# Attention and experts of one layer on one core: the order of score pairs and side operations on TensorE, and the staging of the last expert rounds

## The reference, cut to what matters

```python
Q, K = _apply_rope(Q), _apply_rope(K)                      # 16 heads of 8
scores = einsum('bhqd,bhkd->bhqk', Q, K) / sqrt(8)
attn = softmax(where(causal, scores, -inf))
x = _layernorm(x + (attn @ V) @ o_proj_weight.T)
y = x + _msa(_layernorm(x, ln1_w, ln1_b), w_qkv, w_proj)   # full attention, 16 heads
h = _layernorm(y, ln2_w, ln2_b)
one_hot = one_hot(argmax(h @ gate_w + gate_b), 8)
y = y + sum over e of one_hot[:, e] * (gelu(h @ w1[e]) @ w2[e])   # 128 -> 512 -> 128
out = _layernorm(x + y)
```

## Time and profile before

| | us |
|---|---|
| median of the runs | 973.14 (972.72 to 976.86) |
| the profiled execution | 974.19 |
| its span, first to last instruction | 972.4 |
| first exp to last exp | 41.9 to 873.6 |
| behind the last exp | 98.8 |
| ACT busy | 779.5, of it exps 741.6 |
| ACT idle in front of exps | 87.3 |
| PE busy | 847.0 |

### The profile page before, as it was taken

The page is one execution under the profiler, slowest core; times in us unless marked ns, Lnnn a source line. Parts: engine busy times, 40 slices in busy tenths (PEclk is TensorE's granted clock), DMA queues, the critical chain, the costliest instruction groups (busy, mean ns, idle before and its releaser), DMA issues.

```text
span 972.4 us, 24141 instructions
## 1 busy us (share of the span) xinstructions
PE 847.0 (87%) x9744; PEld 371.3 (38%) x9744; DVE 326.8 (34%) x957; ACT 779.5 (80%) x901; POOL 223.4 (23%) x359
## 2 busy tenths in 40 slices
PE   5689998999999999999989999889999899992261
PEld 2334434344443444333434434434444334442031
DVE  3712614311421034210323322533331633325562
ACT  2468788899999999999989989889989799890340
POOL 4741211111111100000032342033431313321253
PEclk9788999999999999999999999999999999996575
DMA  7975210201110434500100002010000000000101
GB/s 264 274 217 140 88 45 2 88 1 46 45 45 1 101 75 134 172 1 2 45 29 2 2 2 67 7 39 2 3 13 18 29 12 2 2 13 16 38 1 38
DMA packets 34355, 51.58 MB, mean 53 GB/s; under 512 B 4032, under 2 KB 14656, under 8 KB 34240
## 3 DMA queue, kind: packets, MB, share of 16 engines
q1 hardware_dynamic: 32704, 46.30, 16.6%
q0 software_dynamic: 1536, 3.67, 1.2%
HBM read 29.12 MB, written 20.84 MB: 51 GB/s over the span
## 4 chain that ended last, share of the span: by engine, by line
PE 75%; DVE 9%; ACT 7%; issue 4%; DMA 2%; POOL 1%; POOLq 0%; another core or an unknown queue 0%; ACTq 0%; SPq 0%; DVEq 0%
PE ps L447 70%; ACT probs L820 6%; PE ps L452 3%; PE ps L695 2%; ACT squares_blockdiag L857 1%; DVE ln_stats L1010 1%; DVE ln_newton L1003 1%; DMA y_sorted<-early_late 1%; DMA z_rows<-y_sorted,slot_numbers 1%; POOL z_rows L960 1%; DVE squares_blockdiag L1282 1%; DVE ln_newton L1005 0%; DVE ln_newton L1004 0%; DVE z_rows L1019 0%
## 5 line engine op out<-in xcount | busy, mean ns | idle before, releaser
L820 ACT ACTIVATE probs<-ps 128x1024 f32<-128x1024 f32 (+3 forms) x832 | 741.6, 1004 | 87.3 <-PE ps L447 79.6
L447 PE MATMUL ps<-probs,values 128*9 128x256 f32 (+1 forms) x6528 | 438.4, 382 | 1.9 <-DVE q_rotated L1142 1.6
L447 PE MATMUL ps<-query_rows,key_rows 32*128 32x512 f32 (+3 forms) x1664 | 304.4, 491 | 30.7 <-ACT probs L820 26.9
L447 PEld LDWEIGHTS ps<-probs,values 128*9 128x9 f32 x6528 | 144.4, 91 | 192.2 <-issue 92.0
L447 PEld LDWEIGHTS ps<-query_rows,key_rows 32*128 32x128 f32 x1664 | 127.2, 185 | 234.9 <-ACT probs L820 121.2
L919 POOL TENSOR_SCALAR_AFFINE_SELECT probs<-probs 128x256 f32<-128x256 f32 x128 | 53.9, 423 | 246.6 <-ACT probs L820 242.8
L953 POOL COPY parts<-early_late 128x512 f32 x72 | 45.4, 668 | 155.4 <-PE ps L447 155.4
L1142 DVE COPY q_rotated<-ps 128x512 f32<-128x512 f32 x30 | 20.7, 691 | 143.3 <-PE ps L447 127.1
L932 POOL DMA_INDIRECT z_sorted<-z_rows,slot_numbers x16 | 15.7, 981 | 220.9 <-DVE slot_numbers L1272 217.2
L949 POOL COPY parts<-parts 128x512 f32 x72 | 48.0, 710 | 55.7 <-PE ps L447 50.6
L887 ACT ACTIVATE parts<-parts 128x512 f32 x24 | 15.1, 629 | 49.9 <-DVE slot_numbers L1277 28.1
(11 more groups left out here) (155 smaller groups left out, 533.5 us busy)
## 6 DMA issues: line engine op xcount, KB each, us to landing
k_scratch<-parts SPq DMA_DIRECT2D x16, 512.0 KB, 3.8
q_scratch<-parts SPq DMA_DIRECT2D x16, 512.0 KB, 5.1
query_rows<-q_scratch SPq DMA_DIRECT2D x32, 256.0 KB, 5.2
key_rows<-k_scratch SPq DMA_DIRECT2D x20, 256.0 KB, 4.8
key_rows<-k_scratch SPq DMA_DIRECT2D x16, 192.0 KB, 4.3
parts<-in_w SPq DMA_DIRECT2D x1, 2048.0 KB, 8.3
early_late<-in_w SPq DMA_DIRECT2D x8, 256.0 KB, 7.2
early_late<-z_sorted SPq DMA_DIRECT2D x4, 384.0 KB, 3.1
```

Source lines behind the costliest of these rows:

```text
L447: return nc.tensor.matmul(out, l, r, start=start, stop=stop, skip_group_check=True)
L820: nc.scalar.activation(Pr[:, t % 2, 2 * p:2 * p + 2, lo:BLK], score_banks(t, p)[:, :, lo:BLK], ACT.Exp, bias=-SHIFT[r["a"]], scale=SCALE). ...
```

## The change

**The stream.** `run` no longer works by steps but by pairs. `scores` issues one pair. Behind every second pair `late_values` issues the values that are owed, up to the pair three before the newest. A step with side operations issues them behind the first pair that follows a point at which the count `since` is zero; the count starts again behind them. So they stand behind one pair of scores, and the owed values come only after two more pairs. Of a new group the first values are held back until four pairs of it are out where the former group closes in the same batch.

**Places.** Rounds start at steps 24, 30, ..., 54 instead of 26 to 56, with the turn 4 steps later instead of 5. The sorted rows are transposed at steps 21 and 22, not 24 and 25; `post_project` stands at step 6, not 7; `PREP_AT` of block (2, 0) moves by 1 to 2 steps. DVE's `evac` is due half a step later, and the call `due(17)` between `route` and `finish` is gone.

**The tail.** ACT copies `w1` for rounds 0 to 3 at once when the owners of the tiles are known, into `probs`, the values of attention 2 and the old place, and for rounds 4 and 5 behind the tanh of rounds 0 and 1. ACT takes each up's result out of PSUM (Copy) and squares it (Square), with a semaphore `m_x` of its own; DVE's copy and square are gone there. POOL's `w2` copies alternate between two places and wait for the down of two rounds before.

```diff
-UP_AT = (26, 32, 38, 44, 50, 56)
-SORTED_AT = (24, 25)
+UP_AT = (24, 30, 36, 42, 48, 54)
+SORTED_AT = (21, 22)
...
-    (13, 14, 16, 18, 20, 22, (25, 26, 29, 30)),
+    (15, 16, 18, 20, 22, 23, (25, 26, 29, 30)),
...
-IN_SHADE = side_order(UP_AT, 5, 7)
+IN_SHADE = side_order(UP_AT, 4, 7)
...
+def taken(b, name, r):
+
+    if b < NB - 1:
+        return b * OPS + 1 + [(n, q) for _, n, q in IN_SHADE].index((name, r))
+    order = [(n, q) for _, n, q in AT_END]
+    return b * OPS + sum(n != "up" for n, _ in order[:order.index((name, r)) + 1])
+
+
+def issued(b, name, r):
+
+    return b * OPS + 1 + [(n, q) for _, n, q in (IN_SHADE if b < NB - 1 else AT_END)].index((name, r))
...
+        def w2_of(b, r):
+
+            if b < NB - 1 or r % 2 == 0:
+                return w2s
+            return [V[:, g * HID:(g + 1) * HID] for g in range(4)]
+
+        def w1_of(b, r):
+
+            if b < NB - 1 or r == 3:
+                return w1s
+            if r == 2:
+                return [V2[:, g * HID:(g + 1) * HID] for g in range(4)]
+            return [Pr[:, r % 2, g, :] for g in range(4)]
...
-            def side_free(b, k, needs=0):
+            def side_free(b, k, needs=None):
                 turn_taken()
-                pe.wait_ge(m_taken, b * OPS + (k if b < NB - 1 else max(k - 3, needs)))
+                if b < NB - 1:
+                    pe.wait_ge(m_taken, b * OPS + k)
+                    return
+                for name, r in ([AT_END[k - 4][1:]] if k >= 4 else []) + ([needs] if needs else []):
+                    if name == "up":
+                        pe.wait_ge(m_x, r + 1)
+                    else:
+                        pe.wait_ge(m_taken, taken(b, name, r))
...
+            late = []
+
+            def late_values(newest):
+
+
+                closed = False
+                while late and 2 * late[0][0]["t"] + late[0][1] <= newest - 3:
+                    step, p = late[0]
+                    if closed and step["start"] and p == 0 and newest <= 2 * step["t"] + 3:
+                        break
+                    values(step, p)
+                    closed = step["stop"] and p == 1
+                    late.pop(0)
...
+                for n in range(r["k1"] - r["k0"]):
+                    step, pos = run_step(r, n), r["at"] + n
+                    turning = n == TURN_STEP and old is not None and old["closes"]
+                    due = turning or pos in side
+                    for p in range(2):
+                        scores(step, p)
+                        late.append((step, p))
+                        since += 1
+                        if since == 1 and due:
+                            if turning:
+                                turn(old, next((c[1:] for c in reversed(freed) if c[0] < pos), None))
+                            for f in side.get(pos, ()):
+                                f()
+                            since, due = 0, False
+                        if n == TURN_STEP and r["last"] and p == 1:
+                            late_values(2 * step["t"] + p)
+                            general(r["a"], r["qb"], step["t"] + 1)
+                            since = 0
+                        if since == 2:
+                            late_values(2 * step["t"] + p)
+                            since = 0
+                return since
...
-                freed = [(7, post_x, n)]
+                freed = [(6, post_x, n)]
...
+                todo = {5: [lambda: post_turn(n - 1)], 6: [lambda: post_project(n - 1)]}
...
+
+            def stage_up(r):
+
+                for g in range(4):
+                    e = act.value_load(owner[0:1, 4 * r + g:4 * r + g + 1], min_val=0, max_val=E - 1)
+                    nc.scalar.activation(w1_of(b, r)[g], W1[:, bass.ds(e * HID, HID)], ACT.Copy).then_inc(m_w1, 1)
+
             act.wait_ge(m_owner, NB)
+            for r in range(4):
+                stage_up(r)
             for r in range(ROUNDS + 1):
                 if r < ROUNDS:
-                    if r:
-                        act.wait_ge(m_side, (NB - 1) * OPS + 1 + [(n, q) for _, n, q in AT_END].index(("up", r - 1)))
-                    for g in range(4):
-                        e = act.value_load(owner[0:1, 4 * r + g:4 * r + g + 1], min_val=0, max_val=E - 1)
-                        nc.scalar.activation(w1s[g], W1[:, bass.ds(e * HID, HID)], ACT.Copy).then_inc(m_w1, 1)
+                    k = [q[1:] for q in AT_END].index(("up", r))
+                    act.wait_ge(m_side, issued(b, "up", r))
+                    nc.scalar.activation(xg[r % 2], ps[:, side_bank(b, k), :], ACT.Copy)
+                    nc.scalar.activation(tg[:, r % 2, :], ps[:, side_bank(b, k), :], ACT.Square).then_inc(m_x, 1)
                 if r:
-                    tanh(NB - 1, r - 1)
+                    tanh(b, r - 1)
+                if 1 <= r < ROUNDS - 3:
+                    stage_up(r + 3)
...
+                            pool.wait_ge(m_side, issued(b, "up", r - 1))
                         for g, e in enumerate(mine):
                             nc.gpsimd.tensor_copy(w1s[g], W1[:, bass.ds(e * HID, HID)]).then_inc(m_w1, 1)
-                    if r:
-                        pool.wait_ge(m_side, b * OPS + 1 + order.index(("down", r - 1)))
+                    ago = 1 if b < NB - 1 else 2
+                    if r >= ago:
+                        pool.wait_ge(m_side, issued(b, "down", r - ago))
                     for g, e in enumerate(mine):
-                        nc.gpsimd.tensor_copy(w2s[g], W2[:, bass.ds(e * HID, HID)]).then_inc(m_w2, 1)
+                        nc.gpsimd.tensor_copy(w2_of(b, r)[g], W2[:, bass.ds(e * HID, HID)]).then_inc(m_w2, 1)
...
-                link(tt(t, x, x, ALU.mult))
+                if b < NB - 1:
+                    link(tt(t, x, x, ALU.mult))
...
-                    n = b * OPS + k + 1
-                    dve.wait_ge(m_side, n)
+                    if name == "up" and b == NB - 1:
+                        dve.wait_ge(m_x, r + 1)
+                        gelu_arg(b, r)
+                        continue
+                    n = taken(b, name, r)
+                    dve.wait_ge(m_side, issued(b, name, r))
...
-                    events.append((end + 1, lambda r=r: evac(r)))
+                    events.append((end + 1.5, lambda r=r: evac(r)))
...
                     if qb >= 2:
                         add_experts(qb - 2)
                     route(qb - 1)
-                    due(17)
```

More of the change, by code:

```diff
@@ L588, in general, with scores @@
                     pe.wait_ge(s["gen_unit"], (qb + 1) * units)
-            def scores(step):
+            def scores(step, p):
                 r, t = step["r"], step["t"]
-                for p in range(2):
-                    if 2 * t + p:
-                        pe.wait_ge(exp, 2 * t + p)
-                    for hh in range(2):
-                        rows = slice((2 * p + hh) * ROWS, (2 * p + hh + 1) * ROWS)
-                        last = mm(score_banks(t, p)[:, hh, step["lo"]:BLK],
-                                  KAv[rows, r["g"], step["kt"] * P:(step["kt"] + 1) * P],
-                                  QAv[rows, r["qb"] % 2, r["g"], step["lo"]:BLK])
-                    last.then_inc(S_set, 1)
+                if 2 * t + p:
+                    pe.wait_ge(exp, 2 * t + p)
+                for hh in range(2):
+                    rows = slice((2 * p + hh) * ROWS, (2 * p + hh + 1) * ROWS)
+                    last = mm(score_banks(t, p)[:, hh, step["lo"]:BLK],
+                              KAv[rows, r["g"], step["kt"] * P:(step["kt"] + 1) * P],
+                              QAv[rows, r["qb"] % 2, r["g"], step["lo"]:BLK])
+                last.then_inc(S_set, 1)
             def values(step, p):
@@ L684, in m_up @@
                 pe.wait_ge(m_w1, 4 * (b * ROUNDS + r + 1))
-                side_free(b, k, 2)
+                side_free(b, k, ("sorted", 1))
                 for g in range(4):
-                    last = mm(ps[g * TS:(g + 1) * TS, side_bank(b, k), :], slots(4 * r + g), w1s[g])
+                    last = mm(ps[g * TS:(g + 1) * TS, side_bank(b, k), :], slots(4 * r + g), w1_of(b, r)[g])
                 last.then_inc(m_side, 1)
@@ L700, in m_down @@
                 pe.wait_ge(m_w2, 4 * (b * ROUNDS + r + 1))
-                side_free(b, k, 1 + [(n, q) for _, n, q in AT_END].index(("turn", r)))
+                side_free(b, k, ("turn", r))
                 for c in range(TB):
@@ L704, in m_down @@
                         last = mm(ps[g * TS:(g + 1) * TS, side_bank(b, k), 0:D], hTs2[:, c * P + g * TS:c * P + (g + 1) * TS],
[L705 removed]
+                                  w2_of(b, r)[g][:, c * P:(c + 1) * P], c == 0, c == TB - 1)
                 last.then_inc(m_side, 1)
             side_op = dict(sorted=m_sorted_turn, up=m_up, turn=m_hid_turn, down=m_down)
[L710 to L733 removed]
@@ new lines, in _, with run @@
+            late = []
[8 more added lines that the diff above has]
+                    late.pop(0)
```

(14 more changed lines are left out.)

30 lines of the change are left out of this document (3 added, 27 removed).

## The result

| | before | changed |
|---|---|---|
| median of four runs, us | 974.14 (972.72 to 976.86) | 1034.94 (1028.11 to 1036.83) |
| ratio, with its 95% interval | | 1.0602 (1.0558 to 1.0645) |
| profiled span | 972.4 | 1035.1 |
| first exp | 41.9 | 43.2 |
| blocks (1, 0), (1, 1), (1, 2), (1, 3) | 31.6, 63.4, 89.5, 114.2 | 33.1, 79.9, 92.4, 124.2 |

What follows compares the result with a forecast made beforehand. ACT was taken to bound the attention, with PE 0.4 us in reserve per step. Stream +15 and tail -5 on the profiled 974.2 gave 984.2, or 983.1 against the median 973.1; range 962 to 997.

Steps and rivals of the forecast that it cites:

- the price of a lead of 7: Attention: PE has issued seven score pairs up to the owed values; 1.29 us each, high bound about 1.4, low 0.37.
- -2.5 for all taken back by longer overlap: Attention sum: shorter undisturbed runs of exps give back overlap, some 0.6 us a block in attention 2; -2.5 in all.
- The tail: Behind the last exp: earlier w1 copies and denser rounds save 5 us, bounds -3 to -6.
- The counting of leads and the bare price of one: Attention: 106 leads of 6 and 26 of 7 after the change; 0.25 and 1.17 us idle, plus 0.12 overlap each.
- I take 1.29, since ACT's slots, not PE, time the last scores.: Each lead of 7 in attention: the last scores wait for exp k + 3; 1.17 us idle plus 0.12 overlap.
- rival (C): DVE waits behind one score pair cost over 1 us each at post_turn, m_turn, m_gate, m_ranks: 991 us; chance 0.13.
- leads of 6: Attention: six score pairs issued up to the owed values; 0.25 idle plus 0.12 overlap, 0.37 us each.
- it may hold `evac` up ...; I take nothing, since the stop at step 17 covers it: Dropped due(17), blocks (2, 2) and (2, 3): evac held up to 1.5 us, nothing to 3 in all; nothing taken.
- evac's half step: Block (2, 1), step 34: DVE does gelu, which waits for tanh, before evac; 1.1 us.
- so little is gained: Block (2, 1): post_project gives DVE's rows 1.8 us sooner, but PE reaches m_turn about 1.4 us earlier too.
- the same: Block (2, 3): same terms as block (2, 2), with 15.2 us idle before; +3.5 us.
- Rival (E): Side operations behind one pair no longer delay scores; 18 rounds x 0.9 and two big stops go: 949 us; chance 0.06.

Runs made afterwards that it cites:

- e1: The kernel before with the changed kernel's tail alone; ratio to the kernel before 0.9916.
- e9: e8 with values owed by one more pair at 48 quiet places, no side operation inside; ratio to the kernel before 0.9955.
- e10: e8 with values owed by two more pairs at 36 quiet places, no side operation between; ratio to the kernel before 1.0335.
- e12: The changed kernel run again, unedited, on a chip where the kernel before takes 976.5 us; ratio to the kernel before 1.0608.
- e7: The changed kernel with evac's old due time, still without the call due(17); ratio to the kernel before 1.0457.
- e4: The changed kernel with DVE's old order: evac's old due time and the call due(17) restored; ratio to the kernel before 1.032.
- e8: The kernel before, its PE and DVE order kept, with the new step numbers and changed tail; ratio to the kernel before 0.9814.

## Why the prediction was wrong

Its sign was right, its size was not: +10 forecast, +61 measured, outside the range. Two steps failed: the price of a lead of 7 and the nothing put down for DVE's later `evac`. By blocks the attention's forecast and its change in the trace are 0 and +1.5 for (1, 0), -1 and +29.4 for (1, 1) to (1, 3), +5 and +6.3, +7 and +13.7, +3 and +8.4, +3.5 and +7.6 for (2, 0) to (2, 3), with -2.5 for all taken back by longer overlap. The direction of each block of attention 2 came out; attention 1 did not.

- **The tail** held: -5.7 in the trace against -5, in the bounds of -3 to -6; e1 gives -8 (-6 to -10) on another chip. The second up is right behind the first, as foretold:

```profile
979.25 3.64 PE L475 MATMUL ps<-probs,h_cols 128*32 128x512 f32 x16 [1.15 <-DVE early_late L1368]
...
986.46 1.94 PE L475 MATMUL ps<-values,h_cols 128*32 128x512 f32 x8
992.76 1.94 PE L475 MATMUL ps<-parts,h_cols 128*32 128x512 f32 x8
```

  The third up starts 44.4 us behind the last exp, before 50.2.
- **The counting of leads and the bare price of one** held: 26 and 103 stops, 0.25 and 1.17 in the places shown of e9 and e10, where nothing else stands. That two more pairs owed cost this much, with ACT as the bound, was worked out from one row and came true.
- **"I take 1.29, since ACT's slots, not PE, time the last scores."** This step failed, and the term was mis-sized. It is so in e10. In the changed kernel nearly every lead of 7 comes with two operations on one bank with a single score pair between them. Where both are long, PE times the last scores: at step 30 the up takes 1.0 us, one pair of scores 0.5, the wait for DVE's copy 0.55 and the down 1.0, so the last scores start 1.23 us behind where e10 has them (2.40 less 1.17), and I had allowed 0.1. The two `lows` with the same wait lose nothing by it. Over all 26 the stop is 2.06 on the mean: 53.6 us idle, not 30.4. The wait stood in the kernel's own rule, that each operation waits until DVE has emptied the bank, and rival (C) priced it at four places a block only, not inside the rounds. The leads of 6 cost 0.55 instead of 0.25, 30 us more than the bare price; 15 of them, with 18.3 us, also have PE waiting for DVE. They cost 0.52 before as well, so the one row of 0.25 was their floor and not their mean.
- **"it may hold `evac` up ...; I take nothing, since the stop at step 17 covers it"** failed: 13 us. **evac's half step** had no term but 1.1 us in block (2, 1): 14 us, most of it in attention 1, where I forecast -1 and the trace has +29 (+19 in e12; e7, with evac's old time, takes 12 us less there than e12). I looked at what stands ahead of evac on DVE at one boundary of one block; the boundary in (1, 1) had the projection's operations there.
- **The clock in the attention** was not in the sum. Behind the stop of 4.20 us in (1, 1) the half level lasted for 20.5 us, in e12 for 10.2; the block's mean granted clock was 0.81 and 0.91, 0.92 before.
- **"so little is gained"** on `post_project`, and the other step numbers: 10 us were.
- **Two sums** are off. Block (2, 3) is given +3.5 "the same" as (2, 2), but its idle time before is larger, so the same terms give +2.3. Rival (E) counts the two big stops once, 3.3 us, although all three blocks with experts have them. Neither changes the outcome.

What would have caught it: for each batch that holds two operations, walking PE, DVE and PE again, and for each evac listing what DVE has ahead of it.

## What to carry to other kernels

A shared buffer makes the distance between two operations that use it a cost of its own: keep other work between them that takes at least as long as the copy that empties it, and count the operations' own time too. One batch of values between neighbours took back 19 of the stream's 49 us here, not all. An event moved by half a step on an in-order engine is priced by everything it now stands behind, in each stage, not by its half step. And work that is owed to the bound engine has a price which can be read once, where the old order already owes it, and counted from the order. With nothing else there it was 0.28 and 1.4 us for one and two pairs more (e9, e10); two long operations inside the lead come on top.

## What the runs showed of the hardware

**A short DVE instruction can stand for as long as POOL copies.** Of the four last instructions of `finish` in e7, one took 4.04 us, where its kind takes 0.35: it began at 797.98, when POOL began a run of eight copies of 0.60 (798.00), and ended at 802.02, as the seventh did. The same instruction took 4.04 in e12 and 1.82 in the changed kernel's first trace; in e4 and e8 another small one, on 4 elements a partition, took 2.2 and 3.1 in place of 0.17, always beside those copies. DVE's copies out of PSUM were not held up by them: `evac` at 618.1 and 689.7 in the changed kernel ran beside such copies and took its usual 0.69 and 0.68. The Trainium skill (SBUF — State Buffer, "Who interferes with whom") says that a two-port DVE instruction and a GpSimd one take a shared port pair as an exclusive lock and that the second blocks until the first finishes. The traces agree on the blocking, but DVE was held for up to seven GpSimd instructions in a row, not one. Whether this DVE instruction is a two-port one no trace shows, and so that the port pair is the cause is not shown either.

**The chips differ by one stop a block.** The stop of about 2 us while POOL sends rows is in the traces on the two chips that take 974 and 976 us for the kernel before: the changed kernel shows 2.7 at step 16 of (2, 2) and (2, 3) on both. No trace from the three chips at 959 to 960 has it; in e1 blocks (2, 1) to (2, 3) take 131.7, 132.1 and 131.7 us against 135.0, 137.6 and 138.0. Together that is 15.1 us, about the 14.7 by which the kernel before is faster there. The three stops themselves are 6.7 of it (1.96, 2.34 and 2.36); the rest comes behind them. What makes them stays open.
